# Row sums of a graph network: the softmax denominators from two columns of ones behind the 768 features

## The reference

```python
alpha = jax.nn.leaky_relu(qi + kj, NEG_SLOPE)
m = jax.ops.segment_max(alpha, dst, num_segments=n_nodes)
e = jnp.exp(alpha - m[dst])
z = jax.ops.segment_sum(e, dst, num_segments=n_nodes)
a = e / (z[dst] + EPS)
msg = (a[:, :, None] * oj.reshape(-1, heads, out_ch)).reshape(-1, heads * out_ch)
out = jax.ops.segment_sum(msg, dst, num_segments=n_nodes)
```

## Time and profile before

| | |
|---|---|
| median of 3 runs | 2203.03 us (2201.01 to 2203.6) |
| profiled execution, span from first to last instruction | 2198.8 us |
| TensorE matmuls busy (PE) | 1822.8 us, 83% |
| VectorE busy (DVE) | 1519.5 us, 69% |
| GpSimd busy (POOL) | 793.4 us, 36% |
| ScalarE busy (ACT) | 716.5 us, 33% |
| mean granted TensorE clock | 0.903 of full speed |

### The profile page before, as it was taken

The page is one execution under the profiler, slowest core; times in us unless marked ns, Lnnn a source line. Parts: engine busy times, 40 slices in busy tenths (PEclk is TensorE's granted clock), DMA queues, the critical chain, the costliest instruction groups (busy, mean ns, idle before and its releaser), DMA issues. The chain is left out here.

```text
span 2198.8 us, 27805 instructions
## 1 busy us (share of the span) xinstructions
PE 1822.8 (83%) x9161; PEld 1582.8 (72%) x9161; DVE 1519.5 (69%) x2565; ACT 716.5 (33%) x1204; POOL 793.4 (36%) x437
## 2 busy tenths in 40 slices
PE   8995759999999998584647678687999899899976
PEld 3442748898898887574535458676899799799966
DVE  9996667777677765679988886857435543634455
ACT  0213334444443433223326553332222232223120
POOL 1665422332233222237645555630123233333320
PEclk9997879999999999786768888889999999999988
DMA  0003411221222121221120002301222222222230
GB/s 3 19 19 120 141 58 58 64 81 60 62 79 79 51 72 44 79 97 50 46 82 1 0 1 67 106 31 61 62 75 75 75 82 84 72 78 84 91 108 37
DMA packets 43739, 140.34 MB, mean 64 GB/s; under 512 B 4980, under 2 KB 5108, under 8 KB 42356
## 3 DMA queue, kind: packets, MB, share of 16 engines
q1 hardware_dynamic: 35714, 100.03, 14.8%
q10 hardware_dynamic: 7922, 38.96, 4.9%
HBM read 126.39 MB, written 12.58 MB: 63 GB/s over the span
## 5 line engine op out<-in xcount | busy, mean ns | idle before, releaser
L556 POOL TENSOR_TENSOR w_pair<-early,w_pair 128x768 fp32r<-128x768 f32 x234 | 457.9, 1987 | 964.9 <-ACT w_pair L976 964.9
L615 PE MATMUL ps<-w_pair,wide 128*128 128x384 f32 x3168 | 560.9, 337 | 15.2 <-DVE wide L1319 13.8
L615 PEld LDWEIGHTS ps<-w_pair,wide 128*128 128x128 f32 x3168 | 556.3, 190 | 18.3 <-DVE wide L1319 15.5
L615 PE MATMUL ps<-w_pair,cols_x 128*128 128x384 f32 x2448 | 481.6, 358 | 23.6 <-POOL cols_x L556 13.7
L615 PEld LDWEIGHTS ps<-w_pair,cols_x 128*128 128x128 f32 x2448 | 464.1, 205 | 36.2 <-POOL cols_x L556 14.1
L976 ACT ACTIVATE w_pair<-early 128x768 fp32r<-128x768 f32 x234 | 180.6, 838 | 417.9 <-PE ps L615 400.8
L1322 DVE TENSOR_TENSOR early<-early,ps 128x384 f32<-128x384 f32 x176 | 96.1, 549 | 207.0 <-PE ps L615 195.3
L352 PE MATMUL count_ps<-early,src_hot 128*128 (+1 forms) x816 | 179.0, 382 | 7.7 <-DVE early L281 7.6
L976 ACT ACTIVATE early<-ps 128x384 f32<-128x384 f32 (+1 forms) x136 | 67.9, 508 | 290.6 <-PE ps L615 212.6
L352 PEld LDWEIGHTS count_ps<-early,src_hot 128*128 (+1 forms) x816 | 80.1, 98 | 106.1 <-issue 9.2
L913 PE MATMUL ps<-prob,wide 128*128 128x512 f32 x588 | 154.0, 403 | 0.0
(11 more groups left out here) (207 smaller groups left out, 2431.7 us busy)
## 6 DMA issues: line engine op xcount, KB each, us to landing
early<-weights SPq DMA_DIRECT2D x234, 384.0 KB, 3.1
multi<-attn ACTq DMA_DIRECT2D x9, 768.0 KB, 4.5
edge_mask<-counts ACTq DMA_DIRECT2D x13, 512.0 KB, 3.2
kept<-early ACTq DMA_DIRECT2D x3, 1536.0 KB, 6.2
multi<-kept ACTq DMA_DIRECT2D x3, 1536.0 KB, 6.9
counts<-out SPq DMA_DIRECT2D x8, 512.0 KB, 2.6
edge_mask<-masks ACTq DMA_DIRECT2D x7, 512.0 KB, 3.3
yt<-bias_rows ACTq DMA_DIRECT2D x7, 384.0 KB, 4.1
```

What stands on the lines that cost most here:

```text
L556: return nc.gpsimd.tensor_tensor(dst, whole, high.bitcast(F32), ALU.subtract)
L615: mm = nc.tensor.matmul(ps[:, m, 0:HW], left[:, a, k, m * P:(m + 1) * P], w_pair[:, slot_of[0], b, k, :], start=(k == 0 and a + b == 0), s ...
```

## The change

`wide` gets 770 words for each block of nodes instead of 768 (`ROW` = D + 2). The two last words are a column pair: 1.0 in the high part, 0.0 in the low part, written once by VectorE (`ones_columns`): for `wide[0]` and `wide[1]` at the start, ahead of the constants, for `wide[2]` before call 1, as it has held `cols_y` until then. The 8 small matmuls for each `s` are gone. `row_sums` begins with the upper half, now features 384 to 767 and the two columns, 386 columns, and goes on with the lower half of 384. The denominators stand in column 384 of banks 0 to 3, and VectorE reads them when all four banks of the first half are done, before it reads the banks. In call 1 they are read after the bias has been added to the residual. Readers take the upper half first. Counts of `misc_done` are one to four lower.

```diff
+ROW = D + 2
-        wide = [sb(f"wide{i}", [P, 2, KB * N], F32R) for i in range(3)]
+        wide = [sb(f"wide{i}", [P, 2, NB * ROW], F32R) for i in range(3)]
-        rows = [wide[i][:].rearrange("p a (m f) -> p a m f", m=NB) for i in range(3)]
-        cols_y = [wide[i][:].rearrange("p a (k n) -> p a k n", k=KB) for i in (2, 1)]
+        rows_ones = [wide[i][:].rearrange("p a (m f) -> p a m f", m=NB) for i in range(3)]
+        rows = [r[:, :, :, 0:D] for r in rows_ones]
+        cols_y = [wide[i][:, :, 0:KB * N].rearrange("p a (k n) -> p a k n", k=KB) for i in (2, 1)]
...
                 for s in range(NB):
                     pe.wait_ge(x_lo, x_base + s + 1)
                     for m in range(NB):
-                        for a in range(2):
-                            mm = nc.tensor.matmul(ps[:, 5, 2 * m:2 * m + 2], weights_of[:, a, s, m * P:(m + 1) * P], ones[:, 0:2],
-                                                  start=(s + m + a == 0), stop=(s + a == NB), skip_group_check=True)
-                    if s == NB - 1:
-                        mm.then_inc(misc_done, 1)
-                    for m in range(NB):
                         for a, b in ((0, 0), (0, 1), (1, 0)):
-                            mm = nc.tensor.matmul(ps[:, m, 0:HW], weights_of[:, a, s, m * P:(m + 1) * P], source[:, b, s, 0:HW],
+                            mm = nc.tensor.matmul(ps[:, m, 0:ROW - HW], weights_of[:, a, s, m * P:(m + 1) * P],
+                                                  rows_ones[r][:, b, s, HW:ROW],
                                                   start=(s + a + b == 0), stop=(s == NB - 1 and a == 1), skip_group_check=True)
                         if s == NB - 1:
                             mm.then_inc(row_done, 1)
...
-                                                  source[:, b, s, HW:D],
+                                                  rows[r][:, b, s, 0:HW],
...
+            def ones_columns(i):
+                mark(nc.vector.memset(rows_ones[i][:, 0, :, D:ROW].bitcast(F32), 1.0))
+                mark(nc.vector.memset(rows_ones[i][:, 1, :, D:ROW].bitcast(F32), 0.0))
+
             dve.wait_ge(consts, 3)
+            for i in range(2):
+                ones_columns(i)
...
-            def read_denominators(misc, first):
-                dve.wait_ge(misc_done, misc)
-                bank = ps[:, 5, 0:2 * NB:2]
+            def read_denominators(done, first):
+                dve.wait_ge(row_done, done + NB)
+                bank = ps[:, 0:NB, HW]
...
-            read_denominators(45, True)
+            ones_columns(2)
             dve.wait_ge(x_lo, 84)
             add_bias_to_residual(0)
+            read_denominators(0, True)
             invert_denominators(1)
-            norm(0, attention_rows)
+            norm(0, attention_rows, halves=(1, 0))
```

More of the change, by code:

```diff
@@ L750, in _, with row_sums @@
             spread_uv()
-            def row_sums(source, weights_of, x_base, first_sem, first_value, units):
+            def row_sums(r, weights_of, x_base, first_sem, first_value, units):
                 for m in range(NB):
@@ L784, in _ @@
             pe.wait_ge(rows_split, NB)
-            row_sums(rows[0], prob, 80, acc_added, 69, 0)
+            row_sums(0, prob, 80, acc_added, 69, 0)
             pe.wait_ge(acc_ready, NB)
@@ L889, in _ @@
             pe.wait_ge(rows_low, 48)
-            row_sums(rows[0], prob_sets[0], 140, tile_copied, 109, 8)
+            row_sums(0, prob_sets[0], 140, tile_copied, 109, 8)
             pe.wait_ge(den_read, 2)
-            row_sums(rows[1], prob_sets[1], 144, row_read, 13, 16)
+            row_sums(1, prob_sets[1], 144, row_read, 13, 16)
             pe.wait_ge(den_read, 3)
-            row_sums(rows[2], prob_sets[0], 148, row_read, 21, 24)
+            row_sums(2, prob_sets[0], 148, row_read, 21, 24)
             def edge_sums(number, cnt):
@@ L1150, in _ @@
                 act.dma_start(count16[r], counts[SLOT3 + r]).then_inc(cnt_in, 16)
-            for h, turned in enumerate((62, 63, 65, 67)):
+            for h, turned in enumerate((61, 62, 64, 66)):
                 act.wait_ge(misc_done, turned)
                 copy(row_sets[h % 2], ps[0:2, 6 - 2 * (h % 2), :]).then_inc(q_ready, 1)
-            copy_rows(70, 4)
-            copy_uv(71, uv_sets1[0])
+            copy_rows(69, 4)
+            copy_uv(70, uv_sets1[0])
             items = relational_items()
@@ L1202, in _ @@
                         act.dma_start(mask[:], masks[1 + r]).then_inc(mask_in, 16)
-            copy_rows(98, 2)
+            copy_rows(97, 2)
             for r in range(2):
-                copy_rows(100 + 2 * r, 4)
-                copy_uv(101 + 2 * r, uv_sets2[r])
-            copy_rows(104, 4)
+                copy_rows(99 + 2 * r, 4)
+                copy_uv(100 + 2 * r, uv_sets2[r])
+            copy_rows(103, 4)
             for r in range(REL3):
@@ L1210, in _ @@
                     act.wait_ge(x_mid, 144)
-                    copy_uv(105, uv_sets2[0])
+                    copy_uv(104, uv_sets2[0])
                 if r == 2:
@@ L1275, in _ @@
                 if layer == 2:
-                    act.wait_ge(misc_done, 113)
+                    act.wait_ge(misc_done, 109)
                     nc.scalar.activation(v_bc[:], ps[:, 6, :], ACT.Sqrt)
@@ L1610, in count_low, with norm @@
                 sub(prob[:, 1], cnt16, f32(prob[:, 0])).then_inc(cnt_lo, 1)
-            def norm(layer, tile, meanwhile=None):
+            def norm(layer, tile, meanwhile=None, halves=(0, 1)):
                 for u in range(8):
-                    n, m = u // 4, u % 4
+                    n, m = halves[u // 4], u % 4
                     tile(u)
                     mark(nc.vector.bn_stats(bn[:, m, n], acc[:, m, n * HW:(n + 1) * HW]))
-                    if n == 1:
+                    if u >= NB:
                         wait_steps()
@@ L1702, in _ @@
                 source_columns(al1[:, 0, 2, h], h=h)
-            for h, spread in enumerate((64, 66, 68, 69)):
+            for h, spread in enumerate((63, 65, 67, 68)):
                 maxima(spread, mx1[:, 2, h], 18 + h, 84, bank=7 - 2 * (h % 2))
@@ L1758, in _ @@
             source_columns(al1[:, 0, 2, 0])
-            maxima(99, mx1[:, 2, 0], 24, 140)
+            maxima(98, mx1[:, 2, 0], 24, 140)
             relation_uv(1)
@@ L1776, in _ @@
             add_bias_to_residual(1)
-            read_denominators(108, False)
+            read_denominators(24, False)
             invert_denominators(4)
-            norm(1, relation_rows, meanwhile=lambda: count_low(1))
+            norm(1, relation_rows, meanwhile=lambda: count_low(1), halves=(1, 0))
             for m in range(NB):
@@ L1809, in _ @@
                     if layer == 0:
-                        dve.wait_ge(misc_done, 108 + r + 1)
+                        dve.wait_ge(misc_done, 104 + r + 1)
                         mark(nc.vector.tensor_scalar(scale_bc[:, r], ps[:, 6, :], 1.0, None, ALU.max))
```

22 lines of the change are left out of this document (11 added, 11 removed).

## The result

| | before | after |
|---|---|---|
| median of 13 runs each, us | 2203.51 (2197.14 to 2206.25) | 2207.80 (2203.73 to 2213.63) |
| ratio to before, 95% interval | | 1.0023 (1.0014 to 1.0032) |
| span of the profiled execution, us | 2198.8 | 2211.3 |
| mean granted TensorE clock | 0.903 | 0.897 |

The kernel became slower by 0.23%, some 5 us. I had forecast 4.2 us in the other direction, and the time lies above my range. The profiled execution of after is one of its longer ones (2213.1 us), so the two spans differ by more than the medians do.

The account below looks back on a forecast made before the run. It took TensorE, end to end with the ones not hidden, to bound calls 2 and 3. Terms 1.86 + 2.43 + 1.26 - 0.86 - 0.16 - 0.3 gave 4.2 us gain, from 2203.03 to 2198.8 us; range 2195.5 to 2202.6.

Parts of the forecast that it names:

- Layout: Blocks of `wide` at 770 words, low halves and later tensors moved: taken at nothing, bounds 0 and 13.7 ns per odd block.
- Rival C: Later stages: reading odd blocks costs TensorE 13.7 ns on 774 matmuls, 10.6 us in all, giving 2209.4; chance 0.06.
- Ones removed, calls 3 and 4: Second relational layer's `row_sums`: without the ones matmuls, call 3 gains 2.4 us and call 4 1.26 us.
- Call 2: Second relational layer's first `row_sums`: VectorE's weighings delay the denominator read; gain 1.86 us of the 3.4.
- the third case of rival B: Calls 2 to 4: the clock falls once more after a gap of about 1.5 us, costing 1.7; whole rival's chance 0.13.
- my 5.55: Calls 2 to 4 of `row_sums` together: gains of 1.86, 2.43 and 1.26 us.
- Call 1: Attention layer's `row_sums`: TensorE idles 6.1 us instead of 2.7, more time at low clock; 0.86 us lost.
- Memsets: Kernel start: four small memsets on VectorE ahead of the constants TensorE waits for, 0.3 us lost.
- The sum without its layout term: Whole kernel: gains in calls 2 to 4 less call 1, added columns and memsets, 4.2 us gain.
- rival A: Call 1 and later stages: the clock doesn't charge for the pause or wins some back; 2196.2 to 2197.9, chance 0.18.

Follow-up runs that it names:

- a_nolay: The changed kernel's instructions on the layout of before, 386 columns taken from features, so denominators are not sums of ones; ratio to before 0.9966.
- b_base: The kernel before with the three `wide` buffers 16 words longer, blocks still 768 words apart, so low halves and later tensors move; ratio 1.0044.
- b_prob192: The kernel before with 192 unused bytes ahead of `prob`; ratio 1.0054.
- b_prob128: The kernel before with 128 unused bytes ahead of `prob`; one execution, 2216.8 us.
- a_order: The changed kernel with `prob` and `w_pair` allocated ahead of `wide`; ratio to before 1.0011.
- b_wait: The kernel before with VectorE's new order alone: denominators read when all four first-half blocks are in, in call 1 behind the bias; ratio 1.0018.
- a_phase: The changed kernel with `prob` blocks 514 words apart, `prob` and `w_pair` ahead, starts back on multiples of 256 bytes, low halves 32 off; ratio to before 1.0016.
- b_770: The kernel before with the blocks of `wide` 770 words apart; ones, matmuls and waits as before; ratio 1.0046.
- b_best: `b_fill` plus, in each call, the first block's eight ones matmuls issued ahead of the wait for the previous call's accumulators; ratio to before 0.9988.
- b_prob64: The kernel before with 64 unused bytes ahead of `prob`; one execution, 2202.6 us.
- b_fill: The kernel before with twelve matmuls that nothing reads put into the pause of call 1; ratio 0.9998.
- a_nolay_fill: `a_nolay` with 28 unread matmuls in call 1's pause and the denominators read and inverted ahead of the bias; ratio to before 0.9976.
- a_phase_fill: `a_phase` with 28 unread matmuls in call 1's pause and the denominators read and inverted ahead of the bias; ratio to before 0.9991.

## Why the prediction failed, point by point

**The step that failed is "Layout", a term that I took at nothing.** Priced by the table, after loses 2448 x 1.2 ns = 2.9 us in the products, 576 x 5.3 = 3.1 in the heads, 588 x 5.3 = 3.1 in the edge sums, 1.2 in 288 sums of the second relational layer (228.1 to 232.4 ns), and 384 x 2.4 = 0.9 in `row_sums` (the two further columns' 0.8 ns taken off): 11.2 us. Between `a_nolay` and after the ratios differ by 0.0057, 12.6 us. The two agree within the interval, and no other term is needed for after. For `b_base` the same sum is 9.7 us and its ratio gives 9.7. The sum counts every matmul, on the path that ends last or not and at either clock, so it is an upper count, and where the products on `wide` are slow too it comes out above the time: 16 us for `b_prob192` against 12 measured (7.5 to 16.3), 21 for `b_prob128` against 14 in its one execution.

**Rival C had the right kind and the wrong place.** "The read of an odd block costs TensorE time in all later stages" is what happened, and I gave it 0.06. But I tied it to 8 bytes in a 16-byte unit and to the 774 matmuls that load or stream an odd block. The cost is 5 ns a matmul, not 13.7, and falls on even blocks (the first three of each twelve head matmuls, on block 0, take 232.7 ns in after) and on products that read no `wide` at all, because the buffers behind `wide` moved by 192 bytes against the others. The sign I had named, that the edge sums' groups of seven would grow, came: 1.59 to 1.63 us. I had written in the same paragraph that "the low halves and later tensors move", and priced nothing for it. The mean of 403 ns in the earlier trace rows gave no warning: it held no access of the kind. What I had as the argument against, that a weight load overlaps a matmul, doesn't hold for this cost: in `a_order` the heads and edge sums have only their loaded operand moved, and take 232.2 and 231.2 ns instead of 227.0 and 227.4.

**Ones removed, calls 3 and 4: right.** Forecast 18.9 us from start to start and a read after 8.79; measured 19.02 and 8.83 in after, 18.95 in `a_nolay`. Small errors partly cancel. The pause was 0.7 us instead of 0.96: of the 0.85 that I took from the start of call 3, 0.24 lie between VectorE's read and the first matmul there, and between the halves it is 0.04 (the two pieces called issue in the chain of `a_nolay`). A run of matmuls that begins after the pause costs 0.27 more. My 182.5 ns for a row matmul held the 260 ns that the first of each twelve takes behind the ones; without it they are at 173.8. And in after each half is slower by its layout.

**Call 2: the order right, the size wrong in this trace.** VectorE's weighings bounded it, as said. They ended 12.0 us after TensorE's start (1464.8 to 1452.76), against 12.1 before, while the first half took 10.0: the low stretch at its start was about 3 us here (1.00 again from about 1455.9), and 5.8 before. So the pause was 2.71 us, where my 1.5 came from a first half of 11.5. The clock then fell, the third case of rival B, and the second half took 1.5 us more than in call 3. In the traces of `a_nolay` the three calls together gave 5.4 us of my 5.55 (its steps are 2.0 us late at 1441 and 3.4 early at 1515).

**Call 1: right.** Idle 6.07 us (forecast about 6), second half 11.1 (10.9 to 11.0), start to resumption 0.09 us longer (0.1). `b_wait`, whose forecast was 1.0018 to 1.0023, came at 1.0018.

**Memsets: 0.1 instead of 0.3 us.** The four small ones on VectorE start 0.01 to 0.02 us apart, as the timeline of after shows; 0.06 is the duration of one, but not the distance to the next.

```profile
223.78 0.07 DVE L1433 MEMSET wide<- 128x8 f32 x1 [7.49 <-POOL ident L554]
223.79 0.07 DVE L1434 MEMSET wide<- 128x8 f32 x1
223.81 0.07 DVE L1433 MEMSET wide<- 128x8 f32 x1
223.82 0.07 DVE L1434 MEMSET wide<- 128x8 f32 x1
223.88 0.27 DVE L1439 MEMSET yt<- 4x256 f32 x1
```

**The sum without its layout term** was 4.2 us, a ratio of 0.9981. `a_nolay` gave 0.9966 (0.9951 to 0.9980), and with the fill 0.9976 (0.9966 to 0.9985): right in sign, and small rather than large. Where its further 1 to 3 us come from I haven't settled; rival A names one way, and no run isolates it. The lower end of the first interval, 4.4 us, would leave next to nothing to explain, and with the fill the sum would be some 6.7, which the second (3.3 to 7.5) holds.

**What stays open.** Why the place of one operand against the other modulo 256 bytes costs TensorE time. The runs fit a period of 256 bytes, and show that a move of either operand costs, that 64 bytes cost less (+1.6 ns in the edge sums) than 128 and 192 (+5 to +6), and that nothing is lost at the lower clock. They don't show whether it is two reads that meet in one place, and equal steps of 8 bytes on both sides, with the low halves still 32 bytes off (`a_phase`), didn't restore it. Nor do they exclude a small price of its own for a streamed block that starts off a 16-byte boundary: the row sums, which stream `wide`, take 177.0 and 176.6 ns in `b_770` and 175.2 and 174.8 in `b_base`. And one plain repair was not run: blocks 832 words apart (3328 bytes, 13 x 256), which would keep all places modulo 256 and leave room for the ones, at the price of 6144 bytes more in each partition.

## What to carry to other kernels

A few words added to a buffer were not free here even where no instruction read them (`b_base`, `b_prob192`): they moved all that lay behind it. Before such a change, list for each pair of a loaded and a streamed operand the starts and block steps modulo 256 bytes, and after it compare the time per matmul of lines that were not touched. A kernel without the ones matmuls on the old places was the fastest of all (`a_nolay`, 0.9966, which leaves out the columns of ones). Where the places can't be kept, the ones are cheaper to keep and to use: issued ahead of a wait, they fill its pause (`b_best`, 0.9988).

## What the runs showed of the hardware that I had not expected

- A matmul with 512 columns takes 227 ns from start to start when its operands lie equally modulo 256 bytes, and 229, 232.5 and 233.3 when the streamed one lies 64, 128 and 192 bytes further. With 384 columns it is 173.4. There the distance has to be taken with its sign, the streamed start less the loaded one: bytes put ahead of `prob` give +64, +128, +192 in the products (`w_pair` streams), but 192, 128, 64 in the row sums, where `prob` is loaded. Then both go together: 64 costs nothing (173.3 in the products of `b_prob64`, 173.1 in the row sums of `b_prob192`), 128 costs 2 to 3 ns (175.9, 176.1), 192 costs 1 to 3 (174.9, 176.2). On the whole kernel 192 bytes of unused space cost 0.54% (0.34 to 0.74).
- At a granted clock of 0.50 the place makes no difference: 320.0 and 426.7 ns in before, after, `b_prob128` and `b_prob192`.
- With a streamed operand that begins 8 bytes off a multiple of 256, a matmul took 3.6 ns more than expected: 177.8 ns for 386 columns in `a_nolay`, where 173.4 and 0.8 for two columns were to be expected. No run has the two further columns without the 8 bytes on that layout.
- The first run of matmuls after a pause of 0.8 us takes 0.27 us more for the same 48 (8.61 against 8.34), at a granted clock of 1.00: 0.11 from the first to the second, 0.16 at an end that no next matmul covers.
- Pauses of 0.7 to 0.85 us, and one of 1.32 in call 4 of after, left the granted clock at 1.00. After those of 2.65, 2.71 and 6.07 us it fell to 0.50 for a part of what followed, and with the pause filled to 0.56, 0.99 or 1.20 us (`b_fill`, `a_nolay_fill`, `a_phase_fill`) it didn't (8.60, 8.59 and 8.66 us for 48 matmuls instead of 10.21, 10.62 and 10.63).
